# A sort's block tables moved ten groups into its rank loop, and its payload copies moved from VectorE and ScalarE to GpSimd

## The reference

```python
q, k, v = h @ Wq + bq, h @ Wk + bk, h @ Wv + bv        # 8 heads of 8
logits = sum(q[dst] * k[src], axis=-1) * 8 ** -0.5 + edge_attr
attn = segment_softmax(logits, dst)
x = x + segment_sum(v[src] * attn, dst) @ Wo + bo
```

## Time and profile before

| | |
|---|---|
| time, 3 runs | 2752.41 us median (2748.7 to 2753.51) |
| profiled execution | span 3469.1 us; no other time of it is given |
| busy, of that span | PE 58%, PEld 48%, DVE 52%, ACT 33%, POOL 49% |
| first sort in it | to the load of the sorted rows at 920.9 us |

### The profile page before, as it was taken

The page is one execution under the profiler, slowest core; times in us unless marked ns, Lnnn a source line. Parts: engine busy times, 40 slices in busy tenths (PEclk is TensorE's granted clock), DMA queues, the critical chain, the costliest instruction groups (busy, mean ns, idle before and its releaser), DMA issues.

```text
span 3469.1 us, 40007 instructions
## 1 busy us (share of the span) xinstructions
PE 2000.1 (58%) x10636; PEld 1656.2 (48%) x10636; DVE 1794.3 (52%) x6283; ACT 1137.1 (33%) x3025; POOL 1708.5 (49%) x1751
## 2 busy tenths in 40 slices
PE   5655555565335565553496366666666366666766
PEld 4433333343233333332484366566665366666765
DVE  9645454455546776556993243343347233334336
ACT  8322222232104544442113133333334133323333
POOL 0455544545566665663001656556561665655650
PEclk7555555555557777777697566666667566666666
DMA  2000000000222222222002333333342333333331
GB/s 69 3 4 3 4 3 3 4 3 3 76 72 62 63 65 61 64 63 27 1 2 79 96 98 101 101 98 102 96 100 71 100 100 96 102 103 95 103 98 25
DMA packets 114125, 209.58 MB, mean 60 GB/s; under 512 B 46138, under 2 KB 57212, under 8 KB 113532
## 3 DMA queue, kind: packets, MB, share of 16 engines
q0 software_dynamic: 69632, 146.42, 15.6%
q1 hardware_dynamic: 44284, 60.61, 5.7%
HBM read 193.30 MB, written 13.60 MB: 60 GB/s over the span
## 4 chain that ended last, share of the span: by engine, by line
another core or an unknown queue 23%; PE 17%; DVE 12%; issue 8%; ACT 3%; POOL 0%; DMA 0%; DVEq 0%; ACTq 0%; POOLq 0%
PE PS L1391 6%; PE PS L1164 4%; DVE work L1317 3%; PE PS L1401 3%; ACT kv L748 2%; DVE red L1322 2%; DVE work L1309 1%; DVE work L1334 1%; PE PS L760 1%; PE PS L1403 1%; DVE work L739 1%; PE PS L1516 1%; PE PS L1249 1%; DVE work L1038 0%
## 5 line engine op out<-in xcount | busy, mean ns | idle before, releaser
L1297 POOL DMA_INDIRECT arena<-kv_d,S x528 | 516.3, 978 | 338.6 <-DVE work L1334 189.9
L666 POOL DMA_INDIRECT sorted_d<-S,rows x416 | 415.4, 999 | 484.6 <-DVE rows L536 357.8
L1391 PE MATMUL PS<-arena,work 128*128 x1760 | 383.6, 386 | 448.4 <-DVE work L1317 417.8
L1297 POOL DMA_INDIRECT kv<-kv_d,S x352 | 343.2, 975 | 500.1 <-DMA kv_d<-arena 266.9
L1391 PEld LDWEIGHTS PS<-arena,work 128*128 128x128 f32 x1760 | 333.3, 282 | 479.8 <-issue 479.8
L923 POOL DMA_INDIRECT kv<-kv_d,S x440 | 424.6, 965 | 274.5 <-issue 132.5
L1401 PE MATMUL PS<-work,R 128*128 128x128 f32 x1760 | 525.9, 392 | 37.8 <-issue 34.9
L1358 ACT ACTIVATE R<-iota,gate 128x128 f32<-128x128 f32 x880 | 279.8, 388 | 747.8 <-remote 663.1
L1403 PEld LDWEIGHTS PS<-wts,R 128*128 128x128 f32 x1760 | 376.9, 262 | 73.2 <-issue 72.5
L1401 PEld LDWEIGHTS PS<-work,R 128*128 128x128 f32 x1760 | 381.6, 266 | 33.7 <-issue 32.6
L760 PE MATMUL PS<-kv,work 128*128 128x440 f16 x832 | 230.5, 436 | 255.2 <-DVE work L739 179.5
(11 more groups left out here) (272 smaller groups left out, 3361.7 us busy)
## 6 DMA issues: line engine op xcount, KB each, us to landing
work<-segT_d SPq DMA_DIRECT2D x165, 256.0 KB
kv<-kv_d,S POOLq DMA_INDIRECT x792
arena<-kv_d,S POOLq DMA_INDIRECT x528
sorted_d<-S,rows POOLq DMA_INDIRECT x416
kv_d<-arena SPq DMA_DIRECT2D x12, 512.0 KB, 2.9
sorted_d<-S SPq DMA_DIRECT2D x1, 2200.0 KB, 8.5
S<-sorted_d SPq DMA_DIRECT2D x1, 2040.0 KB, 8.8
work<-in_edge_attr_dram SPq DMA_DIRECT2D x1, 1660.0 KB
```

The costliest lines, as they stand in the source:

```text
L666: gp.indirect_dma_start(out=sorted_d, out_offset=bass.IndirectOffsetOnAxis(ap=rows0[0:n, c:c + 1], axis=0), in_=S0[0:n, c, :], in_offset=N ...
L1297: gp.indirect_dma_start(out=ring[s][:, j, :], out_offset=None, in_=kv1_d[l], in_offset=bass.IndirectOffsetOnAxis(ap=S1[:, t, 1:2], axis=0) ...
L1391: done = nc.tensor.matmul(banks[7][:, j * DM:(j + 1) * DM], RT[:, g % 2, j * P:(j + 1) * P], table[:, ds(blocks[g % 3][j] * (3 * DM), DM)] ...
```

## The change

DVE no longer makes the comparison `ge0` and the tables ahead of the rank loop, but inside it, at groups 10 (LATE) and 12, and PE makes the two products they need at group 11. PE no longer waits for the span copy ahead of its first transposes; the product SPAN lies in another bank. All four payload copies go to POOL, behind its constants. POOL clears S0 only after `s_key`. The waits on `s_pay` and `s_paya` move to the stages that need them.

```diff
-        SPAN = banks[6][0:1, 0:HI]
+        SPAN = banks[7][0:1, 480:480 + HI]
...
-        def payload_vector(dve):
-            dve.wait_ge(s_key, 1)
-            dve.wait_ge(s_fill, 16)
-            nc.vector.tensor_scalar(S0[:, 0:EC, 0:1], dst1.unsqueeze(2), 1.0, None, ALU.add)
-            nc.vector.tensor_copy(S0[:, 0:EC, 1:2].bitcast(i32), src1.unsqueeze(2)).then_inc(s_pay, 1)
+        def payload_gpsimd(gp):
+            gp.wait_ge(s_ends, 64)
+            gp.wait_ge(s_attr, 32)
+            gp.wait_ge(s_fill, 16)
+            nc.gpsimd.tensor_scalar(S0[:, 0:EC, 0:1], dst1.unsqueeze(2), 1.0, None, ALU.add)
+            nc.gpsimd.tensor_copy(S0[:, 0:EC, 1:2].bitcast(i32), src1.unsqueeze(2)).then_inc(s_pay, 1)
+            nc.gpsimd.tensor_copy(S0[:, 0:EC - 1, 2:W0P], attr[:, 0:EC - 1, :])
+            nc.gpsimd.tensor_copy(S0[0:TAIL, EC - 1, 2:W0P], attr[0:TAIL, EC - 1, :]).then_inc(s_paya, 1)
...
-            payload_vector(dve)
             dve.wait_ge(s_ohu, NEG)
...
-            vstep(nc.vector.tensor_copy(look[:, 1:2], STARTS))
-            nc.vector.tensor_tensor(ends0, look[:, 1:2], tiles_f, ALU.add).then_inc(s_look0, 1)
-            dve.wait_ge(s_look0, 1)
-            nc.vector.tensor_scalar(ge0, iota_t[0:HI, :], ends0, None, ALU.is_ge).then_inc(s_ge0, 1)
-
-            tables0_vector(dve)
+            nc.vector.tensor_copy(look[:, 1:2], STARTS).then_inc(s_look0, 1)
+
             for g in range(NEG):
+                if g == LATE:
+                    dve.wait_ge(s_look0, 1)
+                    vstep(nc.vector.tensor_tensor(ends0, look[:, 1:2], tiles_f, ALU.add))
+                    nc.vector.tensor_scalar(ge0, iota_t[0:HI, :], ends0, None, ALU.is_ge).then_inc(s_ge0, 1)
+                if g == LATE + 2:
+                    tables0_vector(dve)
...
             pe.wait_ge(s_look0, 1)
-            nc.tensor.matmul(SPAN, look[:, 1:2], ident[0:HI, 0:HI], start=True, stop=True)
-            pe.wait_ge(s_ge0, 1)
-            nc.tensor.matmul(BLOCKS0, ones[0:HI, :], ge0, start=True, stop=True).then_inc(s_blk0, 1)
-            pe.wait_ge(s_span, 1)
             transposes(0, 0)
             for g in range(NEG):
                 b = g % 2
+                if g == LATE + 1:
+                    nc.tensor.matmul(SPAN, look[:, 1:2], ident[0:HI, 0:HI], start=True, stop=True)
+                    pe.wait_ge(s_ge0, 1)
+                    nc.tensor.matmul(BLOCKS0, ones[0:HI, :], ge0, start=True, stop=True).then_inc(s_blk0, 1)
...
+            gp.wait_ge(s_key, 1)
             gstep(nc.gpsimd.memset(S0[:, :, :], 0.0))
```

More of the change, by code:

```diff
@@ L44 @@
 AHEAD = 4
+LATE = 10
 LOW = 2048
@@ L607, in sort_tensor @@
                         transposes(g + 1, 1 - b)
[L609 to L614, removed]
         def lows_scalar(act):
@@ L677, in group_vector @@
         def group_vector(dve):
+            dve.wait_ge(s_pay, 1)
             vstep(nc.vector.tensor_scalar(word_i, src1, 7, None, ALU.logical_shift_right))
@@ L901, in project0_scalar @@
         def project0_scalar(act):
+            act.wait_ge(s_paya, 1)
             for b in range(NB):
@@ L1561, in _ @@
             constants_gpsimd(gp)
+            payload_gpsimd(gp)
             scatters_gpsimd(gp)
@@ L1595, in _ @@
             lows_scalar(act)
-            payload_scalar(act)
             sort_scalar(act)
```

## The result

The changed kernel takes 2744.28 us (median of 8 runs), the kernel before 2751.28 us (8 runs): ratio 0.9973, 95% interval 0.9963 to 0.9982, so 7.0 us faster by the medians and 0.27% by the ratio. That is just beyond the 5.5 us that I had called no measurable change. The forecast of 2751.2 us was 6.9 us too high, inside its range.

A forecast was written before the change was run, and what follows sets the result against it. The prediction took POOL's scatters, which end the first sort, to set the kernel's time. Its terms -2.1 - 7.6 + 5.4 + 3.1 gave -1.2 us, so 2752.4 became 2751.2 us, range 2742 to 2760.

The forecast's parts named there:

- no measurable change: Likeliest rival, chance 0.55: whole kernel at 2751.2 us, two savings worth 9.7 us paid back; 5.5 us counts as no change.
- POOL's scatters end the sort: First sort: POOL's scatters end at 651.4 us, some 14 us after DVE's chain to the projection, and set the time.
- Clearing, -2.1: Kernel start: DVE's masks no longer run beside POOL's clearing, keys then wait for dst's load; -2.1 us, bounds -3.7 and 0.
- Starts first, -7.6: Start of rank loop: PE's first transposes begin at 78.75 us instead of 86.37, all row numbers behind them earlier; -7.6 us.
- Tables in the loop, +5.4: Rank loop, groups 10 to 12: batch 4's row numbers 7.5 us late, so POOL starts it 5.4 us late; bounds 0 and 7.5.
- Payload on GpSimd, +3.1: Histogram: POOL's four copies take 5.0 us and hold DVE, less ACT's 1.9 us; +3.1 us, from 0 to at most 6.6.
- The hold: Histogram: DVE's one-hots stand still while POOL copies the payload; 3.1 us if held, 0 if not.
- ACT's lead of 1.9: Histogram: ACT is one tile pair ahead, 1.9 us, which is taken off the 5.0 us of POOL's copies.
- the sum: All terms of the change together: -2.1 - 7.6 + 5.4 + 3.1 = -1.2 us, giving 2751.2 us.
- Faster: Rival, chance 0.28: rank loop makes row numbers quicker in timed runs, POOL's backlog makes the tables free; 2742.7, with hold 2745.8.
- Slower: Rival, chance 0.17: GpSimd's payload copies cost over 11.7 us of POOL with DVE held; at 17.0 us, 2763.2 us.
- The pauses: Profiled execution of the kernel before: its span exceeds the median by 716.7 us; most pauses were taken to belong to the recording.

The follow-up runs named there:

- a_before_again: The kernel before once more, no edit: 2751.23 us, ratio 0.9999.
- c_payload_only: The kernel before with only the four payload copies moved to GpSimd, tables and clearing as before: 2751.14 us, ratio 0.9999 against the kernel before.
- b: The changed kernel with payload and clearing taken back, so only the tables move into the rank loop: 2745.96 us, ratio 0.9986 against the kernel before.
- l: The changed kernel with LATE = 58 instead of 10 and payload copies back on DVE and ACT: 2743.14 us against 2752.03 for the kernel before, ratio 0.9960.
- d: The kernel before with only POOL's clearing of S0 made to wait for the keys: 2749.33 us, ratio 0.9989 against the kernel before.
- f: The changed kernel with payload copies back on DVE and ACT, in a series with pauses: ratio 0.9969 against the kernel before.
- j: The changed kernel with payload copies back on DVE and ACT, run again in another series with pauses: ratio 0.9973 against the kernel before.
- after: The changed kernel itself, with all parts of the change: 2744.28 us, ratio 0.9973 against the kernel before.

## Why the prediction was right or wrong

*POOL's scatters end the sort: right, and shown.* POOL goes on for 44 us after the last row numbers (608.84 to 653.24), and the load of the sorted rows is issued 1.05 us later (654.29; 1.05 in the kernel before too). Moving a 7.5 us block from before POOL has a backlog to where it has one gave 5.1 us together with the payload's 0.9 (86.59 against 87.51 at the first scatter).

*Clearing, -2.1:* measured -1.8 (7.12 to 5.33) and -2.0 alone. Bound by dst's landing, as said.

*Starts first, -7.6:* measured -7.7 alone, right.

*Tables in the loop, +5.4:* measured 5.8 alone (7.66 gained at the first scatter, 1.90 left at batch 4), and in the changed kernel 8.81 - 3.33 = 5.5. Counted from those of the first group, the row numbers of batch 4 are ready 7.3 us later than in the kernel before (7.5 predicted), and POOL's slack there is 2.07 us (2.1). Right.

*Payload on GpSimd, +3.1: the mechanism right, the size wrong.* The hold is there, yet the first scatter lost only 1.4 us alone (97.75 against 96.32). I had put the hold at the whole of POOL's time, 5.0 us, less ACT's lead of 1.9. POOL needed 6.4 us, but beneath its first operation (2.16 us in the changed kernel) DVE hardly stood: a pair of one-hots took 0.83 us there instead of 0.49, and beneath the second (0.94 us) one took 1.23 instead of 0.69. In all DVE fell 3.4 us behind (35.04 against 31.68), and ACT 1.4. The traces of `a_before_again` and `c_payload_only` also show how DVE made up the rest. Nine groups take 5.76 us while nothing is late, three ACT tiles of 1.92 us each, and 5.43 us behind the hold, where DVE is busy 25.00 of 25.00 us from 35 to 60 us, with 70 instructions instead of 67; so DVE gains 0.3 us every nine groups, and by the end of the histogram it is late only by ACT's 1.4 us.

*What the sum left out.* With these sizes the sum is -1.8 - 7.7 + 5.8 + 1.4 = -2.3 us, and at batch 4 the changed kernel is 3.3 us ahead; two traces of the same kernel differ by 0.4 us at the first scatter (95.90 and 96.32), so I leave the 1 us between the two sums unexplained. At the gather it is 5.4 us ahead. The 2.1 us between lie in three gaps of POOL "for issue", which take 3.65 + 2.98 + 4.50 = 11.1 us in the kernel before and 8.9 in the changed one:

```profile
256.31 0.96 POOL L664 DMA_INDIRECT sorted_d<-S,rows  x1 [2.96 <-issue]
...
404.94 0.95 POOL L664 DMA_INDIRECT sorted_d<-S,rows  x1 [2.98 <-issue]
...
552.47 0.96 POOL L664 DMA_INDIRECT sorted_d<-S,rows  x1 [2.97 <-issue]
```

Whether the change has a part in them stays open. Nothing in it speaks to them, and each trace is one execution; but in the three kernels without pauses that have the tables in the loop (the changed one, `b`, `l`) all nine gaps take 2.96 to 2.98 us, and in the three that have them ahead of it (`a`, `c`, `d`) seven of nine take longer, 3.04 to 4.50. Against an effect of the tables' place: in the series with pauses one gap in `f` and one in `j` take 3.33 and 3.11 us, with the tables in the loop. The other 1.6 us between -5.4 and the median's -7.0 lie inside the interval (-5.0 to -10.2 us); behind the start of the gather the six traces without pauses take 2078.6 to 2089.7 us, a spread of 11 us in stages that no edit touches. So the step that was mis-sized is the payload term, 3.1 us instead of 1.4, and with it went the choice of "no measurable change". Of the measured 7.0 us, 3.3 are shown to come from the change's own steps and 2.1 lie in the open gaps; that the median fell beyond the bound of 5.5 us hangs on these and on the spread.

*The rivals.* "Faster" gave the nearer time (2742.7 to 2745.8), by a mechanism that did not occur: POOL had no backlog at batch 4. Only tables placed where it has one, as in `l`, are free. "Slower" needed 11.7 us of POOL; it was 6.4. The rule of the Trainium skill ("SBUF — State Buffer", section "Who interferes with whom") that a DVE instruction with two SBUF inputs contends with a GpSimd instruction that reads was borne out by the 3.29 us; and the clearing (7.69 to 12.40 us), which only writes, cost the one-hots beneath it nothing to be seen (0.29 and 0.69 us each, as elsewhere). That the loser fully blocks, as the same section of the Trainium skill has it, fits the large copy, and not POOL's first operation, beside whose 2.16 us the one-hots went on.

*The pauses.* Taking them for the recording's was a wrong reading. A time of the profiled execution beside its span would have shown it; for the kernel before none was given. The sum went by the right stretches all the same.

## What to carry to other kernels

Where one engine makes work in batches and another drains it more slowly, side work on the maker is free once the drainer's backlog is longer than that work, and not before: compute the backlog batch by batch. Here it grew by about 1 us a batch, from 0.3 us at batch 4 of the changed kernel to 7.1 at batch 9 and 10.9 at batch 15, against a block of 7.5 us. A per-item cost taken from a trace in which the engine often waited for work is too low if the gaps labelled as waits also hold its own issue gap.

## What the runs showed of the hardware that was not expected

POOL stops for 2.96 to 4.50 us before its 114th, 227th and 340th scatter, each 113 after the last, in all fourteen traces, with and without the pauses (259.77, 408.26 and 557.94 us in the kernel before). No wait explains it and no engine is named, and the 1320 gathers behind the scatters show no such stop in the two traces looked at (`after`, `a_before_again`); what it is stays open. In one series PE, DVE and ACT run without pauses and in another they stand still together, DVE in the rank loop for up to 9 us at a time, on the same kernel and once on the same chip: the kernel before then takes 3442 instead of 2751 us. No experiment here bears on the cause.
